# First cross attention of a two-layer decoder: query and key split into two float32 parts, laid out through device memory and scored in one float32r pass; several copies moved between engines

## The reference, cut to what matters

```python
q = (x1 @ Wq + bq).reshape(Bn, Nq, H, D).transpose(0, 2, 1, 3)   # H=16, D=8
k = concatenate([x2 @ Wk + bk, memory_k], axis=1)                # 128 + 120 keys
v = concatenate([x2 @ Wv + bv, memory_v], axis=1)
attn = softmax(einsum('bhqd,bhkd->bhqk', q, k) * D ** -0.5)
out = (attn @ v heads joined) @ Wp + bp
```

## Time and profile before

| What | Value |
|---|---|
| Median of three executions | 2702.38 us (2698.11 to 2705.56) |
| Span of the profiled execution, first to last instruction | 2695.8 us |
| Difference of the two | 6.6 us |
| PE busy | 2502.7 us, 93% of the span |
| DVE busy | 1849.6 us, 69% |
| ACT busy | 1737.7 us, 64% |
| POOL busy | 1401.1 us, 52% |
| DMA | 151.37 MB, mean 56 GB/s |

### The profile page before, as it was taken

How to read it: one execution, slowest core, us unless ns; L and a number is a source line. 1 busy time by engine, 2 the same in 40 slices (tenths; PEclk the granted TensorE clock), 3 DMA queues, 4 the chain that set the end, 5 groups by cost and what they waited for, 6 DMA issues and landing times. The chain is left out here.

```text
span 2695.8 us, 95989 instructions
## 1 busy us (share of the span) xinstructions
PE 2502.7 (93%) x29950; PEld 2007.2 (74%) x29951; DVE 1849.6 (69%) x5434; ACT 1737.7 (64%) x6375; POOL 1401.1 (52%) x2914
## 2 busy tenths in 40 slices
PE   7999999799999999788889969999999799999995
PEld 6888888577777777487667758888888688888883
DVE  4565555588888888564334448888887388888886
ACT  4666666355555555213556638888888588888883
POOL 2333333233444344165774447777776266666664
PEclk9999999799999999899999979999999899999997
DMA  6332322211111111123332211111111111111100
GB/s 158 100 88 79 89 81 65 65 49 48 49 48 48 48 47 44 37 85 84 78 80 66 66 48 53 47 53 49 50 53 37 33 31 32 31 31 31 31 26 11
DMA packets 270161, 151.37 MB, mean 56 GB/s; under 512 B 51776, under 2 KB 263744, under 8 KB 270016
## 3 DMA queue, kind: packets, MB, share of 16 engines
q1 hardware_dynamic: 261312, 131.57, 18.2%
q0 software_dynamic: 8704, 17.97, 1.9%
HBM read 92.52 MB, written 48.51 MB: 52 GB/s over the span
## 5 line engine op out<-in xcount | busy, mean ns | idle before, releaser
L1187 ACT ACTIVATE pr<-psS,small 128x128 f32<-128x128 f32 x1024 | 366.7, 384 | 95.9 <-DVE small L1258 94.0
L1625 DVE TENSOR_REDUCE small<-psS 128x2 f32<-128x496 f32 x512 | 321.4, 669 | 90.3 <-PE psS L1489 89.1
L1577 ACT ACTIVATE pr<-psT 120x512 f32<-120x512 f32 (+1 forms) x384 | 215.1, 595 | 136.9 <-PE psT L1485 124.5
L1473 PE MATMUL psT<-cross_Qm,cross_xf 32*120 32x512 f32 (+1 forms) x768 | 292.1, 641 | 0.5 <-ACT pr L1577 0.2
L1187 ACT ACTIVATION_READ_ACCUMULATOR pr<-psS,small 128x1 f32 x1024 | 226.1, 221 | 0.0
L1478 PE MATMUL psS<-cross_xf,cross_Qm 32*128 32x248 f32 x1024 | 209.1, 428 | 1.1 <-DVE small L1625 1.1
L2172 POOL DMA_INDIRECT results<-experts_ob,experts_xb x144 | 138.5, 962 | 115.4 <-ACT experts_ob L1992 100.5
L1258 DVE TENSOR_REDUCE small<-psS 128x8 f32<-128x1024 f32 x128 | 156.7, 1224 | 60.5 <-PE psS L1152 60.3
L2112 DVE SCALAR_TENSOR_TENSOR experts_bgh<-experts_bth,psS 128x256 f32<-128x256 f32 x144 | 60.7, 421 | 198.9 <-ACT experts_bth L1984 198.9
L956 POOL TENSOR_SCALAR pr<-pr,small 128x120 f32<-128x120 f32 x512 | 180.4, 372 | 23.3 <-DVE small L910 23.3
L814 ACT ACTIVATE pr<-psS,small 128x120 f32<-128x120 f32 x512 | 179.0, 391 | 5.0 <-DVE small L929 5.0
(11 more groups left out here) (323 smaller groups left out, 8058.1 us busy)
## 6 DMA issues: line engine op xcount, KB each, us to landing
self_parts<-results SPq DMA_DIRECT2D x64, 192.0 KB, 2.4
slots<-blank SPq DMA_DIRECT2D x18, 520.0 KB, 4.5
experts_xb<-slots SPq DMA_DIRECT2D x144, 65.0 KB, 1.9
self_near<-in_x SPq DMA_DIRECT2D x128, 64.0 KB, 1.9
between<-self_xo SPq DMA_DIRECT2D x128, 64.0 KB, 1.6
cross_x<-between SPq DMA_DIRECT2D x128, 64.0 KB, 1.8
cross_res<-between SPq DMA_DIRECT2D x128, 64.0 KB, 1.8
self_x<-in_x SPq DMA_DIRECT2D x64, 64.0 KB, 1.8
```

The source lines that it names most:

```text
L1187: last = act.activation(pr[e.slot % 4][:, cols], K.S[e.slot % 2][:, cols], ACT.Exp, bias=nmax[e.slot % 4][:, n:n + 1], accum_out=tot[k.slo ...
L1473: pe.matmul(to[0:size, :], xf[t.slot][rows(g), every][:, places[ck]], Qm[t.slot][rows(g), :], start=True, stop=False)
L1577: act.activation(PT[k][0:sizes[ck], 512 * n:512 * n + 512], T[turn[2 * r + n]][0:sizes[ck], :], ACT.Exp).then_inc(exped, 1)
L1625: dve.tensor_reduce(nmax[c.slot % 2][:, J * sg[n] + j0:J * sg[n] + j0 + 2], src, AX.X, ALU.max, negate=True).then_inc(maxed, 1)
```

## The change

Query and key rows are permuted by the host (weights, biases and the transposed context), so that row 32j + 8g + d of the projected q and k is channel d of head j of row group g. Each value is split: `high` keeps its upper 20 bits (VectorE, bitwise and), `low` becomes the rest (GpSimd, subtraction). Both, 128 rows of 376 numbers (128 queries, 128 keys, 120 context keys), are stored to device memory (`parts`), and six DMAs bring them back as `pack`: in every row group of 32 partitions, each of the 8 channels has 4 partitions, which hold high/high, high/low, low/high and low/low of query and key; the four heads lie beside each other in the free dimension. A matmul over 32 rows then gives all four products, with the operands declared float32r. `Qm` and its mask are gone; the T matmul of 512 columns becomes four of 128, the S matmuls keep their 248 columns.

```diff
@@ attend_keys_major, SP
-                    a, l, s, o = c + 4, c + 3, c, c - 5
+                    a, l, s, o, e, h = c + 4, c + 3, c, c - 5, c + 1, c + 2
+                    if e.live:
+                        need(sp, T_ps, (e - 4).done(2 * R))
+                        need(sp, parts_out[e.slot], e.p * 32 + 32)
+                        for n in range(4):
+                            to = pack[e.slot][n::4, :, :]
+                            of = K.parts[e.slot].rearrange("(j s) h n -> s j h n", j=J)
+                            if n // 2 == n % 2:
+                                sp.dma_start(to, of[:, :, n // 2, :]).then_inc(pack_in[e.slot], 16)
+                            else:
+                                sp.dma_start(to[:, :, queries], of[:, :, n // 2, queries]).then_inc(pack_in[e.slot], 16)
+                                sp.dma_start(to[:, :, keys], of[:, :, n % 2, keys]).then_inc(pack_in[e.slot], 16)
                     if a.live:
                         need(sp, in_sb, (a - 4).done())
                         need(sp, put_ctx, (a - 4).done())
...
+                        need(sp, v_ps, (a - 4).done())
+                        sp.dma_start(xf[a.slot][:, P:2 * P], D["t_fside"][a.n]).then_inc(f_in[a.slot], 16)
+                    if l.live:
+                        need(sp, parts_out[(l - 2).slot], (l - 2).p * 32 + 32)
+                        sp.dma_start(low[l.slot % 2][:, 2 * P:], D["t_ctxq"][l.n]).then_inc(c_in[l.slot], 16)
...
-                    if l.live:
-                        need(sp, T_ps, (l - 4).done(2 * R, 4))
-                        sp.dma_start(xf[l.slot][:, P:2 * P], D["t_fside"][l.n]).then_inc(f_in[l.slot], 16)
-                        sp.dma_start(xf[l.slot][:, cT], D["t_ctx"][l.n]).then_inc(f_in[l.slot], 16)
+                    if h.live:
+                        need(sp, low_sb, h.done())
+                        sp.dma_start(K.parts[h.slot][:, 0, :], high[h.slot % 2][:]).then_inc(parts_out[h.slot], 16)
+                        sp.dma_start(K.parts[h.slot][:, 1, :], low[h.slot % 2][:]).then_inc(parts_out[h.slot], 16)
@@ TensorE, scores(c, r)
-                            pe.matmul(to[0:size, :], xf[t.slot][rows(g), every][:, places[ck]], Qm[t.slot][rows(g), :],
-                                      start=True, stop=False)
+                            pe.matmul(to[0:size, P * j:P * j + P], pack[t.slot][rows(g), j, places[ck]].bitcast(F32R),
+                                      pack[t.slot][rows(g), j, queries].bitcast(F32R), start=(j == 0), stop=False)
...
+                            last = pe.matmul(to[:, 256 * j:256 * j + CTX + P], pack[c.slot][rows(g), j0 + j, queries].bitcast(F32R),
+                                             pack[c.slot][rows(g), j0 + j, keys].bitcast(F32R), start=True, stop=True)
@@ ScalarE: q and k of c + 2 instead of c + 1; what VectorE did
+                        need(act, parts_out[c.slot], c.p * 32 + 32)
+                        act.activation(low[h.slot % 2][:, 0:P], W0[:, 0:P], ACT.Identity, bias=gbq[:], scale=gain)
+                        act.activation(low[h.slot % 2][:, P:2 * P], W0[:, P:2 * P], ACT.Identity, bias=K.xb[:, 1:2])
...
+                        act.copy(NB[m.slot % 2][:], W0[:]).then_inc(nb_sb, 1)
...
+                        act.copy(oT[n.slot % 2][:], W0[:, 384:512]).then_inc(oT_sb, 1)
+                        act.copy(routed.logits[:, bass.ds(v.n, 1), :].rearrange("p a e -> p (a e)"), W0[:, 256:256 + EXPERTS])
+                        act.copy(xoT[z.slot][:], W0[:, P:2 * P]).then_inc(turned_sb, 1)
@@ VectorE: the four copies and the normalisation are gone, new is
+                        dve.tensor_scalar(high[h.slot % 2][:].bitcast(U32), low[h.slot % 2][:].bitcast(U32), UPPER, None,
+                                          ALU.bitwise_and).then_inc(top_sb, 1)
@@ GpSimd: Qm is gone, new are
+                        pool.tensor_tensor(low[h.slot % 2][:], low[h.slot % 2][:], high[h.slot % 2][:],
+                                           ALU.subtract).then_inc(low_sb, 1)
+                        pool.tensor_scalar(xo[w.slot][:], y[w.slot % 2][:], mv[w.slot % 2][:, 0:1], rs[w.slot % 2][:, 0:1],
+                                           ALU.subtract, ALU.mult).then_inc(normed, 1)
@@ attend_window, SP, at the stage's end
                 sp.wait_ge(late_in, 16 * len(late))
+                sp.wait_ge(K.emptied, 16 * empty.shape[0])
```

More of the change, by code:

```diff
@@ L17 @@
 F32 = mybir.dt.float32
+F32R = mybir.dt.float32r
 BF16 = mybir.dt.bfloat16
@@ L173, in allocate @@
     K.tstep = K.sb("tstep", [P, 3])
+    K.alibi = K.sb("alibi", [P, WH * 48], F32, early)
+    K.Mself = K.sb("Mself", [P, WH * P], F32, early)
+    K.Nself = K.sb("Nself", [P, WH * P], F32, early)
+    K.Gram = K.sb("Gram", [P, 2 * P], F32, early)
+    K.blank = K.sb("blank", [P, BLANKS, ROW], F32, early)
 def set_up(K, D):
@@ L1335, in attend_keys_major @@
     sizes = (CTX, P)
-    places = (slice(0, CTX), slice(CTX, CTX + P))
+    WIDE = 2 * P + CTX
+    queries, keys = slice(0, P), slice(P, WIDE)
+    places = (slice(2 * P, WIDE), slice(P, 2 * P))
+    LOADS = 6 * 16
     S = [K.SS[:, 512 * i:512 * i + 512] for i in range(3)]
@@ L1352, in attend_keys_major @@
         res = [sb(f"res{i}", [P, P]) for i in range(ring)]
-        xf = [sb(f"xf{i}", [P, 2 * P + CTX + P]) for i in range(ring)]
-        qT = [sb(f"qT{i}", [P, P]) for i in range(2)]
-        Qm = [sb(f"Qm{i}", [P, J * P]) for i in range(ring)]
+        xf = [sb(f"xf{i}", [P, 2 * P]) for i in range(ring)]
+        low = [sb(f"low{i}", [P, WIDE]) for i in range(2)]
+        high = [sb(f"high{i}", [P, WIDE]) for i in range(2)]
+        pack = [sb(f"pack{i}", [P, J, WIDE]) for i in range(ring)]
         Vx = [sb(f"Vx{i}", [P, 2, G, P]) for i in range(ring)]
@@ L1381, in attend_keys_major @@
         f_in = [sem(f"f_in{i}") for i in range(ring)]
+        c_in = [sem(f"c_in{i}") for i in range(ring)]
+        parts_out = [sem(f"parts_out{i}") for i in range(ring)]
+        pack_in = [sem(f"pack_in{i}") for i in range(ring)]
+        top_sb, low_sb, v_ps = sem("top_sb"), sem("low_sb"), sem("v_ps")
         xT_out = [sem(f"xT_out{i}") for i in range(ring)]
@@ L1389, in attend_keys_major @@
             "in_sb", "qk_sb", "v_sb", "nb_sb", "exped", "O_sb", "oT_sb"))
-        cleared, ready, masked, put_ctx, split, maxed = (sem(n) for n in (
-            "cleared", "ready", "masked", "put_ctx", "split", "maxed"))
+        cleared, ready, put_ctx, split, maxed = (sem(n) for n in (
+            "cleared", "ready", "put_ctx", "split", "maxed"))
         inverted, scaled = sem("inverted"), sem("scaled")
@@ L1514, in step @@
                     weigh(c - 2, 0)
+                    if h.live:
+                        need(pe, qk_sb, h.done(2))
                     if b.live:
-                        need(pe, qk_sb, b.done(2))
                         need(pe, v_sb, b.done())
@@ L1560, in step @@
                         pe.matmul(W0[:, 0:P], wq, xf[a.slot][:, 0:P], start=True, stop=True)
-                        pe.matmul(W0[:, P:2 * P], wk, xf[a.slot][:, P:2 * P], start=True, stop=True)
-                        pe.matmul(W0[:, 2 * P:3 * P], xf[a.slot][:, P:2 * P], wv, start=True, stop=True).then_inc(proj_ps, 1)
+                        pe.matmul(W0[:, P:2 * P], wk, xf[a.slot][:, P:2 * P], start=True, stop=True).then_inc(proj_ps, 1)
+                    if h.live:
+                        pe.matmul(W0[:, 2 * P:3 * P], xf[h.slot][:, P:2 * P], wv, start=True, stop=True).then_inc(v_ps, 1)
                     if n.live:
@@ L1599, in step @@
+                    if z.live:
+                        need(act, xT_out[z.slot], (z - 4).landed())
+                        act.copy(xoT[z.slot][:], W0[:, P:2 * P]).then_inc(turned_sb, 1)
                     exps(c, 2)
@@ L1647, in step @@
                     if b.live:
-                        need(dve, proj_ps, b.done())
-                        need(dve, qk_sb, b.done(2))
+                        need(dve, v_ps, b.done())
+                        if h.live:
+                            need(dve, qk_sb, h.done(2))
+                        elif w.live:
+                            need(dve, y_ps, w.done())
                         need(dve, O_ps, (b - 4).done(G))
@@ L1742, in step @@
                         pool.tensor_tensor(rs[w.slot % 2][:], ve[w.slot % 2][:], K.half[:, 0:1], ALU.pow).then_inc(lnroot, 1)
+                        need(pool, lnroot, w.done())
+                        need(pool, stored[w.slot], (w - 4).landed())
+                        need(pool, turned_ps, (w - 4).done())
                     if v.live:
```

134 lines of the change are left out of this document (62 added, 72 removed).

## The result

The changed kernel takes **2885.44 us** (median of four runs, 2860.93 to 2890.9) against 2702.35 us (2698.11 to 2705.56) for the kernel before on the same chip: a ratio of **1.0661, 95% interval 1.0617 to 1.0704**, or +183 us. The direction is the forecast's, the size is not: 2717 was forecast, with a range to 2772. The profiled execution took 2890.9 us, with a span of 2889.1.

What follows compares the result with a forecast made beforehand. SP's queue was taken to bound the changed stage at 9.62 us a step against 9.445: about 60 steps give +10.5 us, the stage's ends +4, together +14.5, so 2717 us; range 2675 to 2772.

Steps and rivals of the forecast that it cites:

- What bounds the kernel: Changed stage: TensorE sets the step of 9.445 us before; after the change SP's queue is expected to set it.
- SP's loop, 9.62 us: SP's queue, per step: pack issues to x 2.86, seven others 4.03, loop turn 0.13, two stores landing 2.6 us.
- the seven others: SP's seven DMA issues of a step after the pack issues, up to the stores: 4.03 us with three new waits.
- both rivals that turned on it: SP's wait for stores: landing slow, 10.6 us a step, 2776 us, chance 0.18; landing and issues short, 8.98, 2678 us, 0.20.
- the rival on slow landing: SP's wait for the stores, priced by the 520 KB row: 10.6 us a step, 2776 us, chance 0.18.
- The granted clock: TensorE in the changed stage: a clock below 1.00, which the waits could bring, counted at nothing; listed as a sign of wrong.
- TensorE, 6.9 us a step: Score rounds: float32r at bf16's rate, 0.32 us in place of 0.96, saves 0.64 a round, 2.6 a step.
- The engines' step of 8.3: Changed stage without SP's bound: VectorE's 6.6 us of work plus its idle 1.66 us a step.
- VectorE, ScalarE, GpSimd: Busy time per step after the moved elementwise work: VectorE 6.6, ScalarE 6.8, GpSimd 4.1 us.
- The ends, +4 us: Start and end of the stage: blank stores +1.5, later first scores +5, last steps without pack -2.5 us.
- The rival "SP is no bound", 2638 us: SP's queue: issues go out during the landing, so the engines set the step at 8.3 us; -65 us, chance 0.09.

Runs made afterwards that it cites:

- e8: Kernel before with only the cast, two copies and logits moved to ScalarE and the normalisation to GpSimd: 2695.89 us against 2697.82, ratio 0.9993.
- e1: Changed kernel with its score matmuls declared float32 again, all else kept: 2913.34 us against 2813.7 for the kernel before, ratio 1.0339.
- e3: Changed kernel with pack issued last before the stores, parts stored as broadcasts, pack loaded by one DMA: 2741.93 us against the kernel before's 2813.7, ratio 0.9719.
- e5: e3 with the score matmuls of the first eight sequences in float32: 2613.33 us against 2697.82 for the kernel before, ratio 0.9683.
- e9: The changed kernel itself, run once more: 2994.2 us against 2812.71 for the kernel before, ratio 1.0643.
- e10: Changed kernel with the score matmuls of the first eight sequences in float32, SP's queue as in the change: 2978.75 us, ratio 1.0593 to the kernel before.
- e6: e5 with TensorE held back on purpose at steps 16, 24, 32 and 40 by chained GpSimd memsets: 2862.02 us in one execution, kernel before 2697.8.
- e7: e3 with all score matmuls in float32: 2712.84 us against 2697.82 for the kernel before, ratio 1.0054.
- e11: e3 with the query layout's scores (248 columns) in float32, the keys' layout in one pass: 2779.68 us against 2812.71 for the kernel before, ratio 0.9886.
- e4: Kernel before with scores in one float32r pass over unsplit operands, an extra ScalarE copy of context keys, no pack: 2760.36 us against 2813.7, ratio 0.9795.
- e2: Changed kernel with pack issued last in SP's step, before the two stores: 2953.76 us against 2813.7 for the kernel before, about 1.05.

## Why the prediction was wrong

**What bounds the kernel**: right. TensorE set the step before (e8: taking 1.7 us from VectorE changes nothing), and after the change SP's queue is what makes TensorE wait, at the head of round 0 and for pack.

**SP's loop, 9.62 us**: right in place, short by 1.3 us (10.9 measured). By terms, in the five steps from 848.37 us on (e1's steps from 652 to 989 us give the same within 0.05): from the first pack issue to x 4.2 us against 2.86, since a pack issue takes 0.61 us and follows the last at 0.65, where I took 0.44 to 0.47 from the earlier trace rows, of other copies, and 0.9 more from the sixth to x, where I took 0.66; the seven others up to the first store 4.0 against 4.03; from the first store to the next pack 2.7 against 2.6. The stores land in 1.9 and 2.0 us, against 2.05. So the landing was sized well, both rivals that turned on it fall, and the missed size is the pack issues'. With e1's 10.9 us a step, this error and the later start alone would have given about 1.034 x 2702 = 2794, above my range too. The range was also cut a little short of its own bound: 10.6 us a step is 2776, as the rival on slow landing says, and not 2772.

**The granted clock, "which these waits could bring and which I count at nothing"**: this is the step that failed. It should have been a rival with a price: TensorE waiting 1 to 2.5 us in every step was part of the forecast, and the clock was the only thing by which such waits could cost more than their length. Measured: 13.5 us for 44.5 of 64 steps, +180 us. e3 and e5 show the other side, the same one-pass scores almost without late pack: 7.8 us a step and 3% under the kernel before. The kernel before showed that a pause costs the clock: TensorE is busy for 7.8 of the 20 us before 480, where the stages meet, and the clock is 0.50 until about 510 us. How long it then stays down, under 4 us with float32 scores (e1) and up to 300 us in the change, I had no row to foresee.

The Trainium skill, "TensorE: Matmul & The Clock Gate", section "HAM oscillation — how this bites in real kernels", describes such a case: matmuls broken up by waits for an operand from a DMA lose the clock again and again. The trace agrees, behind the waits of 4.09 and 3.09 us at 584.58 and 909.21. The same page of the Trainium skill, section "What's actually happening", has activity release the throttle. e1 agrees, with its clock back in under 4 us. At the kernel's stretches of 256 and 295 us with TensorE busy throughout and 0.50 granted, the measurement disagrees and decides.

**TensorE, 6.9 us a step**: direction right, size off. The scores of a round take 0.50 us (556.62 to 557.12) and not 0.32, so a round is 0.86, not 0.64, and a step 7.8. The bf16 rate was the wrong end to sit at; why four matmuls of 128 columns take longer than a bf16 one of 512 no run separates. The engines' step of 8.3 was too long: VectorE is busy for 6.5 us of a step of e3, as I had it, but idle for 1.3 and not 1.66, and e3 and e5 run at TensorE's 7.8.

**VectorE, ScalarE, GpSimd**: the and takes 0.35 us (0.55), the subtraction 0.98 (0.83), the cast 0.585 (0.59), the normalisation 0.80, where I had at most 0.46. GpSimd has room for it: e8, which makes the same move, is no slower.

**The ends, +4 us**: the first maxima come 14.4 us later than before (505.9 against 491.5), not 6.5. From the stage's first load to them are 19.1 us against 13.7, so +5.4, where I had +5. SP's queue passes from the blank stores (477.55) to the first load (486.82) in 9.3 us, against 4.0, where I had +1.5. The other 3.7 us are the stage before, which ended later in that execution (the blank stores went out at 477.55 against 473.81; in e9, the same kernel, at 474.05).

**The rival "SP is no bound", 2638 us**: not what the change does, but what it does once SP's queue is relieved. e5 takes 0.9683 x 2702 = 2617.

**Open**: what brings the clock back, and why some waits cost it. The stretches at 0.50 last 256, 14 and 295 us in the change, 68 in e5, 3 to 242 in e10, 14, 198 and more than 300 in e6, nearly all with TensorE busy throughout. Float32 scores have it back in under 4 us (e1) and early in the stage (e7, and e5, e10 and e11 with some of them). The one pass by itself is not the reason, since e4's scores in one pass have it back in about 3 us too, with longer matmuls and no pack. Which property of the work decides, and why e4 loses the clock at waits of 1 us, the runs don't say. No version with e5's start and more room on SP's queue was tried.

## What to carry to other kernels

Before work is taken from the engine that sets the step, work out which queue sets it next and whether the engine will then wait at once for microseconds: a TensorE that is made faster and then waits can lose half of its clock, for far longer than the wait, and end slower than it was. Count every DMA issue of a queue by a row of its own shape, and look at the clock column before the busy share. Where steps can be had slightly slower but never late, they may be the faster ones.

## What the hardware showed

- TensorE busy 100% at a granted clock of 0.50 for 295 us, behind one wait of 3.09 us. With float32 scores waits of 2.98, 2.89 and 2.19 us cost the clock for less than 4 us each, and waits of 0.6 to 1.4 us, one in every step of 10.9 us, left it at 1.00.
- No one length of a wait decides: one of 1.62 us left the clock at 1.00 (e2), and waits of 0.8 to 1.1 us, one in every step of 9.0 us, took it away for some 3 us at a time (e4).
- The length of a DMA issue on SP's queue doesn't follow its size. Medians over the stage are 0.33 to 0.38 us for the other loads of 60 or 64 KB, 0.61 for the pack loads of 64, 124 and 188 KB onto every fourth partition, 0.34 and 0.43 for the two stores of 188 KB, 0.42 for e3's one load of 752 KB.
- Four float32r matmuls of 128 columns in place of one float32 of 512 take 0.50 us against 0.96, about half, and yet not the 0.32 of bf16.
- Four times the DMA traffic cost at most 0.1 us a step: e7 moves 209 GB/s at 9.53 us a step, the kernel before 48 at 9.445.
